# The sorted edge list leaves the setup: layer 0 runs on the edges as given, and the symmetry of the list is checked during layer 1

## The reference

```python
src = concatenate([_s, _d, _loop]); dst = concatenate([_d, _s, _loop])
_o = argsort(dst, stable=True); src, dst = src[_o], dst[_o]

h = relu(layernorm(x))                       # layer 0, four heads
e = concatenate([h[src], h[dst]])            # 206250 x 128
g1 = lrelu(einsum('ef,hgf->heg', e, gate_w1))
a = node_vec[dst] * exp(lrelu(einsum('heg,hog->heo', g1, gate_w2)))
m1 = lrelu(einsum('ef,hgf->heg', e, msg_w1))
beta = lrelu(einsum('heg,hog->heo', m1, msg_w2))
x = x + mean_over_heads(segment_sum(a / rowsum[src] * beta, src))

h = relu(layernorm(x))                       # layer 1
m = (h[src] * sigmoid(f @ prob_w.T) + (f @ review_w.T) * (sigmoid(f @ score_w.T) * w)) * cj[src]
x = x + segment_sum(m, dst) * ci             # f, w: features and weight of the edge
```

## Time and profile before

| | |
|---|---|
| median of 3 runs | 6826.49 us (6826.26 to 6827.18) |
| span of the profiled execution (first to last instruction) | 5851.6 us |
| median less span | 974.8 us |
| busy in the span: PE, DVE, ACT, POOL | 4355.2, 4656.5, 2612.7, 3496.4 us |
| setup, to layer 0's first product | 532.9 us |
| layer 0, to its last gathering of a sum | 3215.6 us |
| middle | 72.7 us |
| layer 1, from its first gather | 2030.4 us |

### The profile page before, as it was taken

One profiled execution on the slowest core, in us unless ns is written; L12 is line 12 of the kernel. 1 busy time (PEld: TensorE's weight loads), 2 busy tenths in 40 slices (PEclk: granted clock), 3 DMA queues, 4 the chain that ended last, 5 costly groups with the idle time before them and its releaser, 6 DMA issues.

```text
span 5851.6 us, 116285 instructions
## 1 busy us (share of the span) xinstructions
PE 4355.2 (74%) x25010; PEld 2801.2 (48%) x25010; DVE 4656.5 (80%) x10137; ACT 2612.7 (45%) x6383; POOL 3496.4 (60%) x3689
## 2 busy tenths in 40 slices
PE   6214999999999999999999999545555555455455
PEld 4212555555555555555555555334444444444444
DVE  9887988989889898988989889756666666666665
ACT  5102777777777777777777777510000000000000
POOL 1002656666565665656656566367777777777776
PEclk9656999999999999999999999855555555555555
DMA  6601333333333333333333333333333323322332
GB/s 247 130 0 47 78 79 80 77 80 79 78 81 78 78 80 78 81 78 78 81 78 80 79 78 80 97 73 59 56 56 56 59 56 56 60 56 56 60 56 51
DMA packets 459109, 437.02 MB, mean 75 GB/s; under 512 B 268369, under 2 KB 340274, under 8 KB 457906
## 3 DMA queue, kind: packets, MB, share of 16 engines
q0 software_dynamic: 122512, 173.81, 18.0%
q1 hardware_dynamic: 308706, 249.41, 15.3%
q10 hardware_dynamic: 27840, 13.23, 1.4%
HBM read 363.27 MB, written 72.83 MB: 75 GB/s over the span
## 4 chain that ended last, share of the span: by engine, by line
PE 46%; POOL 17%; issue 13%; DVE 12%; DMA 6%; ACT 4%; ACTq 1%; SPq 0%; POOLq 0%; DVEq 0%
PE ps_hidden L1814 9%; POOL work L853 9%; PE ps_beta L1866 9%; POOL ends L853 8%; PE ps_hidden L1815 7%; PE ps_beta L1874 7%; DMA ends<-src_table,src_quads 5%; PE ps_alpha L1848 4%; DVE work L1429 4%; DVE work L1317 4%; PE ps_sum L1885 3%; ACT beta_scaled L949 3%; PE ps_T L1803 3%; PE ps_alpha L1857 2%; DVE work L1739 1%
## 5 line engine op out<-in xcount | busy, mean ns | idle before, releaser
L751 POOL DMA_INDIRECT ends<-split_table,src_pairs x1612 | 1581.0, 981 | 1571.7 <-issue 1435.0
L1317 DVE TENSOR_TENSOR work<-work,ps_hidden 128x512 f32<-128x512 f32 x1612 | 1102.3, 684 | 25.4 <-ACT work L897 6.5
L1814 PE MATMUL ps_hidden<-ends_parts,w_high 128*128 128x512 f32 x2418 | 1064.4, 440 | 60.5 <-DVE work L1317 58.8
L897 ACT ACTIVATE work<-ps_hidden 128x512 f32<-128x512 f32 x1612 | 960.6, 603 | 63.2 <-PE ps_hidden L1815 34.6
L1815 PE MATMUL ps_hidden<-ends_hot,window 128*128 128x512 f32 x2418 | 953.4, 394 | 0.0
L853 POOL DMA_INDIRECT work<-src_table,src_quads x808 | 764.4, 946 | 309.2 <-issue 222.0
L853 POOL DMA_INDIRECT ends<-src_table,src_quads x804 | 760.5, 946 | 245.2 <-issue 226.0
L2038 PE MATMUL ps_beta<-work,dst_rows_sb 128*128 128x128 f32 x1608 | 416.4, 441 | 565.6 <-DVE work L1745 565.6
L1115 ACT ACTIVATE ps_alpha<-dots 128x8 f32<-128x8 f32 x403 | 72.7, 180 | 1676.4 <-DVE dots L1707 1676.4
L1866 PE MATMUL ps_beta<-work,msg_w_sb 128*64 128x512 f32 x3224 | 804.1, 609 | 0.4 <-DVE work L1317 0.2
L2038 PE MATMUL ps_beta<-work,equal 128*128 128x128 f32 x1616 | 417.2, 440 | 509.1 <-DVE work L1745 509.1
(11 more groups left out here) (204 smaller groups left out, 6650.2 us busy)
## 6 DMA issues: line engine op xcount, KB each, us to landing
window<-window_table SPq DMA_DIRECT2D x403, 192.5 KB
parts<-in_edge_attr SPq DMA_DIRECT2D x101, 512.0 KB
dst_rows_sb<-by_src SPq DMA_DIRECT2D x403, 128.0 KB
ends<-split_table,src_pairs POOLq DMA_INDIRECT x1612
window_table<-parts SPq DMA_DIRECT2D x49, 386.0 KB, 2.4
sums<-key_rows POOLq DMA_DIRECT2D x403, 32.6 KB
work<-src_table,src_quads POOLq DMA_INDIRECT x808, 2.5
ends<-src_table,src_quads POOLq DMA_INDIRECT x804, 2.5
```

Of the source, the lines that this page charges most:

```text
L751: pool.indirect_dma_start(out=ends[m][:, t, :], out_offset=None, in_=split_table, in_offset=bass.IndirectOffsetOnAxis(ap=src_pairs[m // 2] ...
L897: nc.scalar.activation(scaled[k % NL][:, :], ps_hidden[k % NL][:, :], ACT.Copy, scale=SLOPE).then_inc(scaled_ready, 1)
L1317: nc.vector.tensor_tensor(hidden[k][:, :], scaled[k % NL][:, :], ps_hidden[k % NL][:, :], ALU.max).then_inc(hidden_ready, 1)
L1814: nc.tensor.matmul(o, w1_high[:, k * P:(k + 1) * P], ends_parts[j][:, :], start=True, stop=False)
```

## The change

Layer 0 no longer sorts. It takes the edges as given, sorted by `dst`, and uses each edge (s, d) as if it were (d, s): the near end is `dst`, the far end `src`. That gives the same sums only where the edge list is symmetric. So the windows path is now taken unconditionally, and whether the list is symmetric and the windows fit is found out during layer 1; if not, all engines begin again on the general path behind `fits`, at the end.

- Setup: the list loads, the sort, the four lists in HBM and the branch are gone. `first_near` and `near_offset` come from `dst_all`, by two more conversions on one partition, one more broadcast on PE (L2032), one more subtraction over 1616 columns and three more reductions.
- Setup loop: `copy_low` and the two small columns of a row (`tail_rows`) go to DVE; ACT keeps `copy_column` and `copy_high`. ACT's two `split_table` stores move from behind the loop to behind `copy_high(0)`. PE's broadcasts of the first nodes move behind `project(0)`.
- Layer 0: far indices are loaded as two blocks of `src` (4 numbers a partition and block) instead of 8 numbers in one piece of `by_src_dst`; rows of `dst_rows` replace those of `by_src`. Nothing else is moved on PE, DVE or ACT.
- Layer 1: blocks 6 to 9 make the keys (`key_part`: smaller end, larger end, and the sign of src - dst), blocks 10 to 379 sort them, half a pass a block (`sort_half`, 342 blocks) or, in 28 blocks, half a turning of the list (PE `turn_rounds`, 8 transposes, and ACT `move_rounds`, 2 copies), and blocks 380 to 393 compare the sorted list with its mirror image and set `fits_sb`. The lists lie in `centered` and `table_sb`, which layer 1 does not use. DVE, ACT and PE run layer 1 as one straight stream (`every_block`), POOL and SP keep their loops. SP loads the two lists behind `src_tabled`, ahead of the first x window.
- The built program grows from 6991 to 16154 instructions.

The pieces below are, in this order: ACT in the setup (the turnings, then the loop and what follows it), DVE in the setup (`copy_low`), DVE in layer 1 (`sort_half`, and its place in a block), PE in layer 1 (`turn_round`).

```diff
-            for n, (k, inward, of, _) in enumerate(TURNS[:-1]):
-                for i in range(2):
-                    act.wait_ge(sort_turned, 4 * n + i + 1)
...
             copy_column(0)
             copy_column(1)
             copy_high(0)
+            act.wait_ge(parts_split, 2)
+            act.wait_ge(step, STEPS_TABLE0)
+            act.dma_start(nodes(split_table)[:, :, 0:D], h_parts[0]).then_inc(tables_split, 16)
+            act.dma_start(nodes(split_table)[:, :, D:2 * D + 1], table_sb[:, :, :]).then_inc(tables_split, 16)
             for t in range(NT):
-                copy_low(t)
                 if t + 2 < NT:
                     copy_column(t + 2)
                 if t + 1 < NT:
                     copy_high(t + 1)
-            act.wait_ge(parts_split, 2)
-            act.wait_ge(step, STEPS_TABLE0)
-            act.dma_start(nodes(split_table)[:, :, 0:D], h_parts[0]).then_inc(tables_split, 16)
-            act.dma_start(nodes(split_table)[:, :, D:2 * D + 1], table_sb[:, :, :]).then_inc(tables_split, 16)
             act.wait_ge(zeros_set, 1)
             zero_sums0(0, zeroed)
+            act.wait_ge(high_out[0], 32 * ((NT + 1) // 2))
+            act.wait_ge(high_out[1], 32 * (NT // 2))
+            act.wait_ge(carry_step, 3)
+            copy_ends(0, 0)
...
+            def copy_low(t):
+                for k, n in enumerate((B, HID - B)):
+                    dve.wait_ge(high_taken, 2 * t + k + 1)
+                    if t >= 2:
+                        dve.wait_ge(row_out[t % 2], 16 * (t // 2))
+                    nc.vector.tensor_copy(low_row[t % 2][:, 2 + k * B:2 + k * B + n].bitcast(F32R),
+                                          project_bank(t, k)[:, 0:n]).then_inc(low_ready, 1)
...
+            def sort_half(of, d, run, turned, length, half, steps, moved):
+                wait(dve, sort_moved, moved)
+                dve.wait_ge(sort_step, steps)
+                if run is None:
+                    order_pairs(pairs(1 - of, d)[half], pairs(of, d), turned, (ALU.min, ALU.max)[half])
+                else:
+                    out, given = pairs_of_way(1 - of, d, run, half, length), pairs_of_way(of, d, run, half, length)
+                    order_pairs(out[half], given, turned, ALU.min)
+                    order_pairs(out[1 - half], given, turned, ALU.max)
...
                 nc.vector.tensor_tensor(hot_four[m], columns_ps.unsqueeze(1).broadcast_to([P, T, WIN]),
                                         offset[:, bass.ds(b * T, T)].unsqueeze(2).broadcast_to([P, T, WIN]),
                                         ALU.is_equal).then_inc(hot_ready, 1)
+                check_part(b)
                 dve.wait_ge(gates_ready, b + 1)
...
+            def turn_round(n, i, of):
+                wait(pe, sort_moved, 4 * n + i)
+                for c in range(4):
+                    last = nc.tensor.transpose(turn_bank[:, c * P:(c + 1) * P],
+                                               runs[of][:, (4 * i + c) * P:(4 * i + c + 1) * P], ident[:, :])
+                last.then_inc(sort_turned, 1)
```

1148 lines of the change are left out of this document (591 added, 557 removed).

## The result

The changed kernel takes 6369.45 us (median of 4 runs, 6366.97 to 6387.79) against 6826.84 us of the kernel before: ratio 0.9334, 95% interval 0.9321 to 0.9348. That is 457 us faster where 338 were forecast, and outside the range.

A forecast was written before the change was run, and what follows sets the result against it. Bounds taken: the sort on the path to layer 0, PE in layer 0, POOL's gather stream in layer 1. Terms -339 + 0 + 0 + 1 = -338 gave span 5513.6 and time 6488.5 us; range 6455 to 6560.

The forecast's parts named there:

- Times outside the span: Whole kernel: the 974.8 us between profiled span (5851.6 us) and median (6826.5 us) were taken as constant.
- My rival that it shrinks with the span: Whole kernel: time outside the span is proportional to the span, 918 us instead of 974.8; time 6432 us, chance 0.06.
- Setup: From start to first product: sort, lists and branch go, first product at 194.1 us against 532.9, -338.8 us.
- the turn: Setup's projection loop: with low copies on DVE a turn falls from 2.80 to 2.5 us, bounds 2.42 and 2.80.
- the zero stores at the end: End of setup: five zero stores from ACT's queue in the way of the first window, 2.2 us added.
- The bound for the first product: End of setup: first product between 181 us (loop at 2.42) and 220 us (loop at 2.8, stores kept apart).
- Layer 0: Layer 0: same instructions on PE, ACT and DVE, PE the bound; cost 0, bounds -5 and +10 us.
- Layer 1: Layer 1: POOL's gathers stay the bound and DVE's added 441 us of sorting is hidden; cost 0.
- VectorE's cover: Layer 1: DVE's 1.77 us of waiting a block hides 1.29 us of added sorting, with 0.6 us left.
- The lock: Layer 1: sort instructions with two SBUF inputs stop POOL's descriptor writing, adding 441 us; 6929 us, chance 0.07.
- The evidence against it: Layer 1: L1348, with two SBUF inputs, took 0.28 us within a 0.95-us gather; gathers beside busy DVE took 0.943 to 0.962.
- the tail (+1): End of kernel: `fits_sb`, its load and a branch on five engines, about 1 us; general path not run.

The follow-up runs named there:

- e3: Changed kernel without the check in layer 1 (no keys, sort, turnings or comparison; flag set in the setup), still one straight stream: 6477.4 us.
- e4: Changed kernel without the check, and with DVE, ACT and PE in layer 1 back in loops of eight blocks: 6489.5 us.
- e16: Changed kernel without the check, plus one VectorE instruction with two SBUF inputs over 1024 columns in each of blocks 10 to 379: 5624.2 us.
- e17: Changed kernel without the check, plus one VectorE reduction with one SBUF input over 1024 columns in each of blocks 10 to 379: 5532.2 us.

## Why the prediction was wrong

1. **Times outside the span: the step that failed.** "I take the difference, 974.8 us, as constant: no row explains it." It was no time outside the span but another level of the same kernel, 206 us in layer 0 and 773 in layer 1, and it isn't constant under the change. Of the 119.7 us by which the gain was undersized, layer 1 has 123.7 and layer 0 33.0, less 37.6 by which the setup's gain was oversized. Layer 1's part comes with the check (e3, e4: 83 to 97 us more without it), whose index loads are less late; why the level exists stays open. A difference of 14% between profile and timing should have been a case with a wide range of its own, not a constant. My rival that it shrinks with the span (6432 us, at 0.06) had the right sign by luck: at level U span and time agree, so there is no time outside to shrink.
2. **Setup, -338.8 forecast, -301.2 measured.** The terms that were mis-sized: the turn (2.75 us, not 2.5; 2.80 was in the bounds), the eleven turns beside the table stores and the first gathers (27 us more than at 2.75, 6 of them level U's), and the zero stores at the end. With them the last row landed about 40 us later than the 186 taken. The bound for the first product (181 to 220) was missed: 233.1, 227.1 at level L.
3. **Layer 0, 0 forecast**: -12.0 at level L, where the quad's period went from 31.85 to 31.7 us; -33 at level U. I didn't test why.
4. **Layer 1, 0 forecast**: +97.3 at level L. VectorE's cover held: its idle time before the three products is 1.03 us a block, more than the 0.6 forecast, and it never became the bound. The lock, which I priced at all of 441 us or nothing, exists and costs 95 (the changed kernel's profile at level U has 80 us of such excess too). The evidence against it was read wrongly: L1348 inside a gather shows only that a gather *already started* is left alone. The gathers of layer 1 that were beside a busy VectorE never began inside a long instruction with two SBUF inputs, since layer 1 had none (L1733 has one of its in PSUM). That gathers can be held at all stood in that profile and was not read: layer 0's took up to 1235 ns (L751), 401 of the 1612 over 1 us, where the earlier trace rows has 962 at most.

```profile
L751 POOL DMA_INDIRECT ends<-split_table,src_pairs x1612: 942/953/1235, 523.8 to 3722.1; - x180
```

Which instruction holds those gathers I have not traced. It is not this lock alone: most are longer by 0.11 us, and began beside VectorE instructions with one input in PSUM. The price per start should have been a term of the sum: the 342 blocks have 1.2 to 1.3 us of such instructions each, 327 gathers began inside one, and each lost the rest of it less 0.13 us, 0.26 us on average. A small reading was off too: 0.8 MB is the size of each of the two lists, not of both, which cost nothing visible.
5. **At level L the forecast would have been** 5841.5 - 338 = 5503.5 of span against 5624.5: wrong by the lock (97) and the setup (37), less layer 0's 12.
6. The middle (0) was right within 1 us; the tail (+1) lies inside layer 1's stretch and isn't measured apart; the list is found symmetric and the general path isn't run.

## What to carry to other kernels

If the profile's span is far from the timed runs, find out which execution the profile is of before costing a change: profile the kernel in the same session, and look for an engine whose register instructions have grown. Before VectorE work is put beside a stream of indirect DMAs, count how many gathers will start inside an instruction with both inputs in SBUF; keep one input in PSUM, or use a reduction with one input, if it can be had; a `tensor_scalar` from SBUF to SBUF in its fast form held a gather as well. When a copy is moved off a ring of engines that wait for each other, follow the ring without it once round before taking the next engine's busy time as the new period.

## What I had not expected of the hardware

- A gather on GpSimd is held at its start by a VectorE instruction with two SBUF inputs, for the rest of it less 0.13 us; in layer 1 it is not held by one that begins after it, nor by a reduction with one input (e16, e17: excess 97.4 and 1.2 us for 370 instructions of 1.21 us).
- One program has two levels, 5843 to 5849 and 6755 to 6833 us, by session. At the upper one SyncE's register instructions take 335 ns on average in layer 1 instead of 43, many of them 0.7 us, as long as POOL gathers and up to 2.5 us behind.
- At the upper level an order of loads is worth 152 us (133 to 152) that is worth nothing or costs 40 to 50 us at the lower one.
